# Two edge passes of a graph kernel: the block numbers of a chunk read into PE registers once instead of twice

## The chip, the cores and the metric

The kernel runs on one core of a Trainium2 chip, as one program from input to output. The metric is the device time of one execution in microseconds (us), lower is better. A core has five engines that run side by side, each with its own stream of instructions and its own sequencer, and meet only through semaphores: PE (TensorE, matmuls), DVE (VectorE), ACT (ScalarE), POOL (GpSimd, here above all the gathers) and SP (SyncE, which issues the plain DMAs).

## The reference

The program is a two-layer model on a graph of 6250 nodes, 256 features and 106,250 edges sorted by their target node. Each layer has a graph stage and a feed-forward stage. Two stages matter here. They have the same form: a score for every edge and head, a softmax of the scores over the edges of one target node, and a sum of messages, weighted with it, into that node.

```python
# layer 0: attention
score = einsum('ehd,ehd->eh', K[src], Q[dst]) / sqrt(HD) + edge_bias
m = segment_max(score, dst);  ex = exp(score - m[dst])
attn = ex / segment_sum(ex, dst)[dst]
out = segment_sum(attn[:, :, None] * V[src], dst)
# layer 1: the same with another score
scores = leaky_relu(s_src[src] + s_dst[dst], 0.2)
out = segment_sum(hh[src] * alpha[:, :, None], dst)
```

## The kernel before, in words

The nodes lie in blocks of 128. The edges are cut into **steps**: a step is a tile of 128 edges together with one block of target nodes, so that its sum goes into one block. There are 880 steps, in 55 **chunks** of 16 (`CH`), a chunk in four **quarters** of 4 steps. Which block a step belongs to is data: an earlier stage writes the numbers into `g.step_block`, one row of 32-bit integers in SBUF. An engine that needs them reads them into registers with `step_range` and computes an address from each.

Pass 1 is `attend_edges` (layer 0), pass 2 is `edges` (layer 1). Both run the same pipeline over the chunks. In one turn three chunks are under way: chunk c is scored, chunk a = c - 1 goes through the softmax, chunk b = c - 2 is multiplied out and added to its nodes. What PE does in a turn, in an order written out by hand:

- `place_t` (L440, L944) spreads the target lanes of a quarter over the partitions; ACT makes the transposed one-hot matrix `sel_t` of it (L581, L1069).
- The look-up of chunk c multiplies `sel_t` with the rows of the step's block. This is the matmul that needs a block number. In pass 1 it is `query` (L452), one for each pair of steps, eight a chunk; in pass 2 it is `at_node` (L953), one for each quarter, with four small matmuls.
- Softmax of chunk a: the scores turned (L475, L974), `row` (L479 to L481, L978 to L980), `ends` (L485, L486, L984, L985), `weights_of` (L490, L989) and the correction of what is summed so far (`at_node` L495 in pass 1, `shrinks_of` L994 in pass 2). Between them DVE scans maxima, subtracts (L750, L1231), and ACT takes the exponent (L607, L1125), copies the weights (L614, L1130), makes the one-hot matrix `sel` (L589 and L592, L1078 and L1081) and the denominators (L598, L1087).
- `add_up` of chunk b (L468, L967): one matmul of 264 columns in f32 a step, into one of two banks of PSUM in pass 1 and three in pass 2. It waits until DVE has added what stood in the bank before. DVE adds each result to its block (L785, L1266); it reads the block numbers into registers of its own, and that is not changed.

An f32 matmul shows as two records. POOL issues one gather a step (L427, L931), into a ring of 44 steps in pass 1 and of 4 chunks in pass 2, and waits until `add_up` has freed the place.

Before, PE reads the numbers in halves of eight (`U`): `blocks_of(c, half)`. The first half of chunk c + 1 is read near the end of turn c and handed to the next turn as `ahead`; the second half of chunk c is read in the middle of turn c. In pass 1 the two loads stand between `add_up(b, 10, 11)` and `add_up(b, 12, 13)`, and between `ends(a)` and `add_up(b, 4)`. In pass 2 they stand between `add_up(b, 12, 13, 14)` and `weights_of(a)`, and between `add_up(b, 6, 7)` and `add_up(b, 8)`. In the profile both are PE's sequencer's work and have no row.

## Time and profile before

| | us |
|---|---|
| time, median of 3 runs (lowest to highest) | 5473.58 (5453.67 to 5479.73) |
| span of the profiled execution | 5404.7 |
| the profiled execution's own time | not listed apart from the three above |
| PE matmuls busy | 3933.5 (73%) |
| DVE busy | 3064.0 (57%) |
| POOL busy | 2464.9 (46%) |
| ACT busy | 1859.8 (34%) |

The page lists for each engine what share of the span it was busy, and cuts the span into 40 slices. The whole span mixes stages with different limits: the two edge passes are about half of it. A timeline row gives the start of an instruction or of a merged run of equal ones, how long it took, its engine and line, what it writes and reads, and in brackets how long the engine had idled before it and who ended that. Matmul starts are recorded, their ends are modelled.

### The profile page before, as it was taken

What the parts mean: (1) busy time and instruction counts of PE and PEld (TensorE: products, weight loads), DVE (VectorE), ACT (ScalarE), POOL (GpSimd) and SP (SyncE); (2) the same over time, 40 slices, a digit from 0 to 9 for tenths busy, and PEclk for the clock granted to TensorE, in tenths of its full rate; (3) what the DMA queues carried; (4) which work ended last, traced back from release to release, by engine and by line L of the source; (5) the groups of instructions that cost most, each with busy time, mean ns of one, the idle gap of its engine ahead of it and who ended that gap; (6) DMA issues with size and microseconds to landing.
All of it is one profiled execution on the core that took longest, in us unless ns stands there. A gap on an engine that the chain in (4) does not pass through costs nothing. (4 is left out here: it accounts for less than half of the span.)

```text
span 5404.7 us, 69347 instructions
## 1 busy us (share of the span) xinstructions
PE 3933.5 (73%) x16281; PEld 2847.1 (53%) x16282; DVE 3064.0 (57%) x7623; ACT 1859.8 (34%) x5073; POOL 2464.9 (46%) x2442
## 2 busy tenths in 40 slices
PE   6867777777777659967853666666666338999999
PEld 4545555555555448856732444444444226777776
DVE  3278887878888766662154666666667773111111
ACT  1333333333333312311222444444444322333332
POOL 2256665656666450001166666666663422333332
PEclk8988988888888879977986788777887559999999
DMA  2555555555555232211173333333331451111111
GB/s 80 186 146 149 154 151 148 151 140 153 147 148 151 83 118 84 91 55 40 52 252 89 95 96 96 94 95 94 93 96 47 127 194 20 32 32 31 31 31 27
DMA packets 316127, 553.64 MB, mean 102 GB/s; under 512 B 63431, under 2 KB 213783, under 8 KB 315857
## 3 DMA queue, kind: packets, MB, share of 16 engines
q0 software_dynamic: 137120, 388.63, 27.4%
q1 hardware_dynamic: 178736, 161.98, 9.8%
q8 instruction: 100, 1.64, 0.1%
q14 instruction: 171, 1.39, 0.1%
HBM read 459.75 MB, written 90.62 MB: 102 GB/s over the span
## 5 line engine op out<-in xcount | busy, mean ns | idle before, releaser
L427 POOL DMA_INDIRECT attend_ring<-kv_rows,all_step_src x880 | 860.1, 977 | 624.5 <-PE attend_ps_agg L468 371.3
L931 POOL DMA_INDIRECT edge_ring<-head_rows,all_step_src x880 | 878.7, 999 | 457.1 <-issue 204.2
L967 PE MATMUL edge_ps_agg<-edge_msg,edge_sel 128*128 128x264 f32 x1760 | 676.3, 520 | 188.9 <-issue 57.3
L468 PE MATMUL attend_ps_agg<-attend_msg,attend_sel 128*128 128x264 f32 x1760 | 605.1, 445 | 179.7 <-DVE graph_qa L785 122.9
L967 PEld LDWEIGHTS edge_ps_agg<-edge_msg,edge_sel 128*128 128x128 f32 x1760 | 414.5, 257 | 328.2 <-issue 198.7
L1266 DVE TENSOR_TENSOR graph_acc<-graph_acc,edge_ps_agg 128x264 f32 x880 | 369.9, 420 | 367.2 <-PE edge_ps_agg L967 169.0
L2821 DVE TENSOR_TENSOR moe_gl<-moe_ps_h,moe_act 128x341 f32<-128x341 f32 x210 | 107.8, 514 | 776.8 <-PE moe_ps_h L2739 776.8
L452 PE MATMUL attend_ps_q<-graph_qa,attend_sel_t 128*128 x1760 | 527.7, 429 | 27.4 <-ACT attend_sel_t L581 17.8
L785 DVE SCALAR_TENSOR_TENSOR graph_qa<-graph_qa,all_step_same,attend_ps_agg 128x264 f32 x880 | 421.1, 479 | 170.1 <-remote 121.0
L468 PEld LDWEIGHTS attend_ps_agg<-attend_msg,attend_sel 128*128 128x128 f32 x1760 | 329.3, 208 | 347.2 <-issue 148.6
L2739 PE MATMUL moe_ps_h<-experts_w,moe_xt 128*128 x1680 | 501.7, 451 | 0.6 <-ACT moe_xt L2770 0.6
L589 ACT ACTIVATE attend_sel<-all_lane,all_step_dst 128x128 f32<-128x128 f32 x880 | 281.1, 390 | 498.5 <-PE attend_ps_agg L468 232.4
L2693 POOL DMA_INDIRECT out<-moe_y,moe_to_row x105 | 166.8, 1588 | 579.4 <-ACT moe_y L2779 567.5
L452 PEld LDWEIGHTS attend_ps_q<-graph_qa,attend_sel_t 128*128 128x128 f32 x1760 | 377.0, 217 | 99.7 <-issue 31.6
L2739 PEld LDWEIGHTS moe_ps_h<-experts_w,moe_xt 128*128 128x128 f32 x1680 | 311.1, 190 | 146.4 <-issue 2.8
L1254 DVE TENSOR_TENSOR edge_msg<-edge_ring,edge_prob 128x256 f32<-128x256 f32 x880 | 345.1, 414 | 32.0 <-issue 17.6
L1069 ACT ACTIVATE edge_sel_t<-edge_ps_gt 128x512 bf16<-128x512 f32 x220 | 130.5, 593 | 576.5 <-DMA tab_rel_x<-tab_rel_x 402.8
L1078 ACT ACTIVATE edge_sel<-all_lane,all_step_dst 128x128 f32<-128x128 f32 x880 | 279.1, 389 | 125.4 <-PE edge_ps_agg L967 86.6
L680 DVE TENSOR_TENSOR attend_prod<-attend_ps_q,attend_ring 128x512 f32<-128x512 f32 x440 | 297.7, 677 | 40.8 <-remote 30.2
L2724 PE MATMUL moe_ps_y<-experts_w,moe_gt 128*128 x1260 | 309.9, 387 | 0.7 <-ACT moe_gt L2796 0.7
L1825 PE MATMUL ffn_ps_h<-ffn_xt,ffn_wa 128*128 128x256 f32 x1216 | 272.3, 383 | 11.8 <-ACT ffn_xt L1848 11.8
L1867 ACT ACTIVATE ffn_ht<-ffn_ps_h,ffn_ba 128x256 f32<-128x256 f32 x304 | 144.2, 474 | 364.2 <-PE ffn_ps_h L1825 364.2
(424 smaller groups left out, 6587.9 us busy)
## 6 DMA issues: line engine op xcount, KB each, us to landing
attend_ring<-kv_rows,all_step_src POOLq DMA_INDIRECT x880
edge_ring<-head_rows,all_step_src POOLq DMA_INDIRECT x880
kv_rows<-qkv_kv SPq DMA_DIRECT2D x25, 512.0 KB, 2.9
experts_w<-in_w_t SPq DMA_DIRECT2D x16, 682.0 KB
attend_mask<-run_starts SPq DMA_DIRECT2D x440, 8.1 KB
edge_mask<-run_starts SPq DMA_DIRECT2D x440, 8.1 KB
head_rows<-hds_hh SPq DMA_DIRECT2D x25, 264.0 KB
qkv_x<-in_x SPq DMA_DIRECT2D x25, 256.0 KB, 3.3
```

The source lines that it names most:

```text
L427: nc.gpsimd.indirect_dma_start(ring[:, step % RING1, :], None, g.kv_rows, bass.IndirectOffsetOnAxis(g.step_src[:, step:step + 1], 0)).then ...
L452: ins = nc.tensor.matmul(ps_q[k % QBANKS][:, i, :], sel_t[:, q % 2, u % QU, :], queries[:, bass.ds(blocks[u % U], 1), :].rearrange("p b d ...
L468: nc.tensor.matmul(ps_agg[i % SUM_BANKS][:, 0:AGG], sel[:, q % 2, u % QU, :], msg[:, q % 2, u % QU, :], start=True, stop=True).then_inc(s_ ...
L589: ins = nc.scalar.activation(sel[:, q % 2, u, :], g.lane[:], ACT.Square, bias=g.step_dst[:, step:step + 1], scale=-1.0)
L680: nc.vector.tensor_tensor(prod[:, at:at + 2, :], ps_q[k % QBANKS][:], ring[:, first:first + 2, 0:D], ALU.mult).then_inc(s_prod, 1)
L785: nc.vector.scalar_tensor_tensor(at[u % U], at[u % U], g.step_same[:, i:i + 1], ps_agg[i % SUM_BANKS][:, 0:AGG], ALU.mult, ALU.add).then_i ...
L931: nc.gpsimd.indirect_dma_start(ring[:, n % slots, u, :], None, g.head_rows, bass.IndirectOffsetOnAxis(g.step_src[:, step:step + 1], 0)).th ...
L967: nc.tensor.matmul(ps_agg[i % BANKS][:, 0:AGG], sel[:, q % 2, u % QU, :], msg[:, q % 2, u % QU, :], start=True, stop=True).then_inc(s_agg, 1)
L1254: nc.vector.tensor_tensor(msg[:, q % 2, u % QU].rearrange("p (h c) -> p h c", c=HC)[:, :, 0:HD], ring[:, b % slots, u, 0:D].rearrange("p ( ...
L1266: nc.vector.tensor_tensor(at[u % U], at[u % U], ps_agg[i % BANKS][:, 0:AGG], ALU.add).then_inc(s_add, 1)
L2724: last = nc.tensor.matmul(ps_y[:], gt[0:size, c, :], w2[0:size, :, c, :][:, bass.ds(e, 1), :].rearrange("p a d -> p (a d)"), start=(c == 0 ...
L2739: last = nc.tensor.matmul(ps_h[2 * i + hf][:, 0:EHALF], xt[:, slot, k, :], w13[:, :, k, i, hf * EHALF:(hf + 1) * EHALF][:, bass.ds(e, 1), ...
```

## The change

Both passes: `blocks_of` takes no half any more and reads all 16 numbers of a chunk; a look-up takes its number by the step's own place in the chunk and not by its place in the half. One call a turn is left, for chunk c + 1. In pass 1 it stands after the last query of the turn (`query(c, 7, ...)`), ahead of `add_up(b, 10)`. In pass 2 it stands after the last look-up (`at_node(c, 3, ...)`), ahead of `place_t(c + 1, 0)`. The order of all else is the same. The 16 registers are held until the last look-up of the next turn.

```diff
--- before.py
+++ after.py
@@ -450,7 +450,7 @@
                 for i in range(2):
                     u = pair * 2 + i
                     ins = nc.tensor.matmul(ps_q[k % QBANKS][:, i, :], sel_t[:, q % 2, u % QU, :],
-                                           queries[:, bass.ds(blocks[u % U], 1), :].rearrange("p b d -> p (b d)"), start=True, stop=True)
+                                           queries[:, bass.ds(blocks[u], 1), :].rearrange("p b d -> p (b d)"), start=True, stop=True)
                 ins.then_inc(s_q, 1)
 
             def add_up(b, *steps):
@@ -494,14 +494,14 @@
                 pe.wait_ge(s_rs, a * quarters + 1)
                 nc.tensor.matmul(shrinks, sel[:, 0, 0, :], shrink[:], start=True, stop=True).then_inc(s_shrink, 1)
 
-            def blocks_of(c, half):
-                return step_range(nc, g, mybir.EngineType.PE, c * CH + half * U, U)
+            def blocks_of(c):
+                return step_range(nc, g, mybir.EngineType.PE, c * CH, CH)
 
             pe.wait_ge(s_set, SET_OPS)
             pe.wait_ge(s_made, 2)
             place_t(0, 0)
             place_t(0, 1)
-            ahead = blocks_of(0, 0)
+            ahead = blocks_of(0)
             query(0, 0, ahead)
             query(0, 1, ahead)
 
@@ -522,35 +522,31 @@
                     query(c, 3, ahead)
                 if a is not None:
                     ends(a)
-                if c is not None:
-                    blocks = blocks_of(c, 1)
                 if b is not None:
                     add_up(b, 4)
                 if c is not None:
-                    query(c, 4, blocks)
+                    query(c, 4, ahead)
                     place_t(c, 3)
                 if b is not None:
                     add_up(b, 5, 6)
                 if a is not None:
                     weights_of(a)
                 if c is not None:
-                    query(c, 5, blocks)
+                    query(c, 5, ahead)
                 if b is not None:
                     add_up(b, 7)
                 if c is not None:
-                    query(c, 6, blocks)
+                    query(c, 6, ahead)
                 if after:
                     place_t(c + 1, 0)
                 if b is not None:
                     add_up(b, 8, 9)
                 if c is not None:
-                    query(c, 7, blocks)
+                    query(c, 7, ahead)
+                if after:
+                    ahead = blocks_of(c + 1)
                 if b is not None:
-                    add_up(b, 10, 11)
-                if after:
-                    ahead = blocks_of(c + 1, 0)
-                if b is not None:
-                    add_up(b, 12, 13)
+                    add_up(b, 10, 11, 12, 13)
                 if after:
                     query(c + 1, 0, ahead)
                     place_t(c + 1, 1)
@@ -951,7 +947,7 @@
                 pe.wait_ge(s_rt, c * quarters + q + 1)
                 for u in range(QU):
                     ins = nc.tensor.matmul(ps_sd[:, q * QU + u].rearrange("p h a -> p (h a)"), sel_t[:, q % 2, u, :],
-                                           dst_parts[:, bass.ds(blocks[(q * QU + u) % U], 1)].rearrange("p b h a -> p (b h a)"),
+                                           dst_parts[:, bass.ds(blocks[q * QU + u], 1)].rearrange("p b h a -> p (b h a)"),
                                            start=True, stop=True)
                 ins.then_inc(s_sd, 1)
 
@@ -993,18 +989,17 @@
                 pe.wait_ge(s_rs, a * quarters + 1)
                 nc.tensor.matmul(shrinks, sel[:, 0, 0, :], shrink[:], start=True, stop=True).then_inc(s_shrink, 1)
 
-            def blocks_of(c, half):
-                return step_range(nc, g, mybir.EngineType.PE, c * CH + half * U, U)
+            def blocks_of(c):
+                return step_range(nc, g, mybir.EngineType.PE, c * CH, CH)
 
             pe.wait_ge(s_set, SET_OPS)
             pe.wait_ge(s_made, 3)
-            for half in range(2):
-                blocks = blocks_of(0, half)
-                for q in (2 * half, 2 * half + 1):
-                    place_t(0, q)
-                    at_node(0, q, blocks)
+            blocks = blocks_of(0)
+            for q in range(quarters):
+                place_t(0, q)
+                at_node(0, q, blocks)
             place_t(1, 0)
-            ahead = blocks_of(1, 0)
+            ahead = blocks_of(1)
 
             def turn(c, a, b, ahead):
                 after = c is not None and c + 1 < count
@@ -1025,26 +1020,21 @@
                 if a is not None:
                     row(a)
                 if b is not None:
-                    add_up(b, 6, 7)
-                if c is not None:
-                    blocks = blocks_of(c, 1)
-                if b is not None:
-                    add_up(b, 8)
+                    add_up(b, 6, 7, 8)
                 if a is not None:
                     ends(a)
                 if c is not None:
-                    at_node(c, 2, blocks)
+                    at_node(c, 2, ahead)
                     place_t(c, 3)
                 if b is not None:
                     add_up(b, 9, 10, 11)
                 if c is not None:
-                    at_node(c, 3, blocks)
+                    at_node(c, 3, ahead)
                 if after:
+                    ahead = blocks_of(c + 1)
                     place_t(c + 1, 0)
                 if b is not None:
                     add_up(b, 12, 13, 14)
-                if after:
-                    ahead = blocks_of(c + 1, 0)
                 if a is not None:
                     weights_of(a)
                 if b is not None:
```

## Rows read from the trace of the kernel before

**Rows 1.** Stages: start:end, length, each engine's busy time, granted clock, DMA.

```profile
core 0: us, PE busy (x) PEld busy (x) DVE busy (x) ACT busy (x) POOL busy (x), PEclk, DMA share, GB/s
...
290.00:1830.00 1540.00, 1115.18 (x4317) 797.89 (x4317) 1245.24 (x2617) 591.92 (x1657) 929.91 (x896) 0.88 0.53 147
...
2900.00:4190.00 1290.00, 840.80 (x3511) 555.00 (x3509) 854.19 (x2665) 584.81 (x1680) 815.36 (x815) 0.79 0.34 90
```

**Rows 2.** Once a turn, by line: count, duration min/median/max, first and last start.

```profile
L490 PE MATMUL attend_ps_tp<-all_ident,attend_prob_t x55: 327/328/477, 294.1 to 1840.2; 128*128 128x128 f32 x55
...
L989 PE MATMUL edge_ps_tp<-all_ident,edge_prob_t x55: 272/418/476, 2892.5 to 4168.9; 128*128 128x128 f32 x55
```

**Rows 3.** Timeline of PE, opening of pass 2.

```profile
2824.05 0.70 PE L953 MATMUL edge_ps_sd<-edge_dst_parts,edge_sel_t 128*128 x4 [0.77 <-ACT edge_sel_t L1069]
2825.23 0.59 PE L944 MATMUL edge_ps_gt<-edge_feat,all_lane_feat 128*128 128x512 bf16 x1 [0.48 <-issue]
2826.59 0.57 PE L953 MATMUL edge_ps_sd<-edge_dst_parts,edge_sel_t 128*128 x4 [0.77 <-ACT edge_sel_t L1069]
2827.01 0.59 PE L944 MATMUL edge_ps_gt<-edge_feat,all_lane_feat 128*128 128x512 bf16 x1
```

**Rows 4.** Timeline of PE, one turn of pass 1.

```profile
1002.25 0.69 PE L468 MATMUL attend_ps_agg<-attend_msg,attend_sel 128*128 128x264 f32 x2
...
1010.01 1.03 PE L452 MATMUL attend_ps_q<-graph_qa,attend_sel_t 128*128 x4
1010.88 0.61 PE L468 MATMUL attend_ps_agg<-attend_msg,attend_sel 128*128 128x264 f32 x2
...
1013.03 1.32 PE L468 MATMUL attend_ps_agg<-attend_msg,attend_sel 128*128 128x264 f32 x4 [0.38 <-DVE graph_qa L785]
```

**Rows 5.** Timeline of DVE, the same turn.

```profile
1012.41 0.48 DVE L785 SCALAR_TENSOR_TENSOR graph_qa<-graph_qa,all_step_same,attend_ps_agg 128x264 f32 x1
```

**Rows 6.** Timeline of PE, one turn of pass 2.

```profile
3644.32 2.85 PE L967 MATMUL edge_ps_agg<-edge_msg,edge_sel 128*128 128x264 f32 x6
...
3647.64 0.38 PE L944 MATMUL edge_ps_gt<-edge_feat,all_lane_feat 128*128 128x512 bf16 x1
```

**Rows 7.** PE by line, 2900 to 4190 us: busy, mean, idle before.

```profile
L944 PE MATMUL edge_ps_gt<-edge_feat,all_lane_feat 128*128 128x512 bf16 x210 | 99.3, 473 | 0.2
```

**Rows 8.** Timeline of all engines, end of a turn of pass 2.

```profile
3629.32 0.56 PE L953 MATMUL edge_ps_sd<-edge_dst_parts,edge_sel_t 128*128 x4 [3.61 <-ACT edge_sel_t L1069]
...
3629.91 0.38 PE L944 MATMUL edge_ps_gt<-edge_feat,all_lane_feat 128*128 128x512 bf16 x1
...
3630.14 2.83 PE L967 MATMUL edge_ps_agg<-edge_msg,edge_sel 128*128 128x264 f32 x6
...
3631.39 0.39 DVE L1266 TENSOR_TENSOR graph_acc<-graph_acc,edge_ps_agg 128x264 f32 x1
3631.72 0.27 DVE L1231 TENSOR_TENSOR edge_less<-edge_ps_tp,edge_most 128x128 f32<-128x128 f32 x1
3632.02 0.31 ACT L1125 ACTIVATE edge_prob_t<-edge_less 128x128 f32<-128x128 f32 x1 [1.10 <-DVE edge_less L1231]
...
3632.76 0.42 PE L989 MATMUL edge_ps_tp<-all_ident,edge_prob_t 128*128 128x128 f32 x1
...
3636.40 1.39 PE L967 MATMUL edge_ps_agg<-edge_msg,edge_sel 128*128 128x264 f32 x4 [1.74 <-issue]
```

**Rows 9.** Timeline of ACT, the turn of rows 6.

```profile
3652.38 0.60 ACT L1069 ACTIVATE edge_sel_t<-edge_ps_gt 128x512 bf16<-128x512 f32 x1 [3.68 <-DMA tab_rel_x<-tab_rel_x]
```

**Rows 10.** ACT by line: 2900 to 4110 us, then 4110 to 4190 us.

```profile
L1069 ACT ACTIVATE edge_sel_t<-edge_ps_gt 128x512 bf16<-128x512 f32 x202 | 119.8, 593 | 482.6 <-DMA tab_rel_x<-tab_rel_x 381.1 <-PE edge_ps_gt L944 81.1 <-issue 20.2
...
L1069 ACT ACTIVATE edge_sel_t<-edge_ps_gt 128x512 bf16<-128x512 f32 x8 | 4.7, 590 | 8.5 <-PE edge_ps_gt L944 8.4
```

**Rows 11.** The gathers of pass 2 by line, and POOL's idle before them.

```profile
L931 POOL DMA_INDIRECT edge_ring<-head_rows,all_step_src x880: 952/960/1412, 2795.9 to 4118.0; - x176
...
  PE edge_ps_agg L967: 157.6, 177
```

## The prediction

> **What bounds the kernel now.** The change touches two stages, so I read the stage table first and not the whole span. Pass 1, `attend_edges`, fills 290 to 1830 us and pass 2, `edges`, fills 2900 to 4190 us; in pass 1 DVE is busy 1245 of 1540 us and PE 1115, in pass 2 no engine is above two thirds [rows 1]. Each pass runs 55 turns, and an operation that runs once a turn gives the turn: (1840.2 - 294.1) / 54 = 28.6 us in pass 1 and (4168.9 - 2892.5) / 54 = 23.6 us in pass 2 [rows 2]. Pass 2 is therefore a chain across engines, where one microsecond added at the right place costs 50. Then I read the timeline of PE around each of the four places where block numbers are read, and beside it DVE and ACT.
>
> A register load is not an instruction that the profile counts as busy, so it shows only as a hole on PE, where nothing covers it. The opening of pass 2 has one such hole. The opening does place, look up, place, look up for the four quarters of chunk 0. Where no load stands between look-up (L953) and place (L944), place starts 2827.01 - 2826.59 = 0.42 us after look-up. Where the second load of eight stands, it starts 2825.23 - 2824.05 = 1.18 us after, with 0.48 us of it marked idle [rows 3]. **A load of eight registers pushes back what follows by about 0.75 us.** It is the same seam (L953, load, L944) at which the change puts its new load in pass 2.
>
> **Pass 1, load removed after `ends`.** It stands between L486 and step 4's L468. PE's L468 at 1002.25 has no idle before it [rows 4]: the sequencer reads registers while PE still works off what is queued, the queries ahead of `ends` above all. Nothing is gained; without that cover the load would have cost 0.75 us.
>
> **Pass 1, load removed between steps 11 and 12.** PE idles 0.38 us before step 12's L468 at 1013.03, released by DVE's L785 [rows 4]. DVE adds step 10 from 1012.41 for 0.48 us, and only its end (1012.89) frees the bank of step 12; DVE did not idle before it [rows 5]. So the load is hidden by DVE, and 0 is gained. Bound below zero: if the 0.38 us were the load's after all, 53 x 0.38 = 20 us.
>
> **Pass 1, new load of 16 between query 7 and step 10.** Query 7 keeps PE from 1010.01 until step 10 starts at 1010.88 (0.87 us of cover), and DVE takes step 10 at 1012.41, 0.92 us after PE ended it at 1010.88 + 0.61 = 1011.49 [rows 4, 5]. A load that pushes back by 0.75 to 1.5 us shows up to 0.6 us on PE and none of it on DVE. Step 11 waits for DVE's add of step 9, which the load doesn't touch. Cost 0. Pass 1 in sum: 0, bounds -20 and +10 (0.2 us a turn, if some turns lack the cover).
>
> **Pass 2, load removed between steps 7 and 8.** PE runs steps 6, 7, 8 as one block of 2.85 us from 3644.32 with no idle in it [rows 6]: in all that time two matmuls a step are queued and the load runs beside them. Gain 0.
>
> **Pass 2, load removed between step 14 and `weights_of`.** PE runs steps 12, 13, 14 as one block of 2.83 us from 3630.14, then L989 at 3632.76 without idle [rows 8]. Gain 0.
>
> **Pass 2, new load of 16 between the last look-up and `place_t(c + 1, 0)`.** Here PE has no cover: look-up (L953) at 3629.32 follows an idle of 3.61 us, and L944 (3629.91) and step 12 (3630.14) follow it without a gap [rows 8]; over the stage L944 waited 0.2 us in 210 runs [rows 7]. So the whole push-back appears. For 16 registers it is at least the 0.75 us of eight and at most twice that, 1.5 us; no row here splits the 0.75 us into a fixed part and a part per register. I take 1.1, the middle. What is queued behind the load on PE: L944, steps 12 to 14, L989, step 15, L994. Who waits:
> - ACT's L1069, which answers L944; the next on ACT is L1125 (3632.02), after 1.10 us idle and itself later by then, so this is covered.
> - DVE's add of step 12, at 3631.39. A third of PE's block of 2.83 us is one step, so step 12 is done at 3630.14 + 0.94 = 3631.08 and DVE has it 0.3 us later [rows 8]. Part of the 0.3 is the signal's way, so the cover is 0 to 0.3 us; I take 0.2. Where the clock is granted in full the steps are done sooner and the cover is larger; its mean here is 0.79 [rows 1].
> - Behind that add, in DVE's fixed order, stands L1231 (3631.72), for which ACT idled 1.10 us (L1125, 3632.02). ACT then has two one-hot groups, `prob` and the denominators to make, and for these PE's first step of the next turn (3636.40) idles 1.74 us [rows 8]. Nothing on this chain has slack.
>
> So each turn grows by 1.1 - 0.2 = 0.9 us. 52 turns have both the load and a chunk being added: 52 x 0.9 = 47 us. Bounds: 52 x (0.75 - 0.3) = 23 and 52 x 1.5 = 78 us. The openings trade two loads of eight for one of 16, under 1 us. The number of address calculations, of matmuls and of DMAs is the same.
>
> The Trainium skill, "Runtime: NRT & Kernel Launch", section "Instruction fetch mechanics", gives about 200 ns for each register loaded, also in bulk; by it eight would take 1.6 us and 16 3.2 us. The row's 0.75 us for eight speaks against that size here, though that page speaks of loads from HBM. "DMA: Bandwidth & Descriptors", section "Latency and other measured facts", gives a floor of about 600 ns for a load; if the load were all floor, the new one would push back by the 0.75 us of the old, and the sum would be its lower bound.
>
> **Sum.** Span 5404.7 + 47 = 5451.7 us. The profiled execution's own time is not listed; the three runs lie 49 to 75 us above its span. I set the sum on the median: 5473.6 + 47 = 5520.6 us.
>
> **Rivals.**
> 1. *Absorbed, no change.* Twice a turn ACT and DVE idle for a signal of PE that comes long after the work: L944 runs at 3647.64 for 0.38 us, but ACT's L1069 starts at 3652.38 after 3.68 us idle [rows 6, 9]. Such waits (the name "tab_rel_x" in the row is a wrong guess of the releaser) are 381.1 us of ACT's idle in 202 runs of L1069 [rows 10]. In the last turns, after the last gather was issued at 4118.0, L1069 idles 8.5 us in 8 runs and never for that name [rows 10, 11]. So these waits belong to the gathers and not to PE's own order. If their end is set by the gathers' pace, 0.9 us more in front of them only shortens them: 0 to 15 us in all, 5480. For it: no row explains them. Against it: L931 itself idles for PE 157.6 us [rows 11], so gathers follow PE, and the chain from the look-up at 3629.32 to the next turn at 3636.40 lies outside them [rows 8].
> 2. *Twice the price.* The 16 numbers come as two loads, or the time goes with the count: 52 x (1.5 - 0.2) = 68 us, 5541.
> 3. *Faster: one late signal goes with one load.* The late signal at 3652.38 follows the first look-up after the load between steps 7 and 8 [rows 6, 9], and there are two loads and about two such waits a turn. If the load is their cause, one of two goes, from the turn in which the second load is gone: half of 381.1 = 190 us less, and 47 more, 5330. Against it: the last turns have both loads and hardly any late signal [rows 10]. Its mild form is that the 20 us of pass 1 are real and pass 2 is absorbed: 5454.
>
> **How the numbers follow.** Forecast (23 to 60 us slower) 0.47; absorbed 0.27; twice the price or pass 1 hit too 0.12; mild gain 0.10; a late signal gone 0.04. 0.5% is 27 us, about what a measurement can tell from no change. The forecast's lower end lies inside it, which gives slower 0.57, within 0.33, faster 0.10. The range takes in the mild gain in part and the double price: 5460 to 5555. The forecast alone spans 5497 to 5534.
>
> **What would show each step.** In pass 2's opening, and after each last look-up, L944 with an idle of about 1 us that was not there: the new load; its length is the price. L989 from first to last 47 us longer, its 55 runs 24.5 us apart. The idle before ACT's L1125 up from 1.1 to 2.0 us. In pass 1, L490 first to last the same within 10 us, and L468 at step 12 still idle 0.38 us for L785. The forecast is wrong if the waits at L1069 shrink by what L944 gains, or if L944's new idle is under 0.5 us.

## The result, and the profile after

The kernel after takes 5454.36 us (median of 20 runs, 5419.99 to 5469.84), the kernel before 5469.55 us (20 runs, 5453.67 to 5496.9). The ratio is 0.9969, with a 95% interval of 0.9955 to 0.9982: 17 us less (10 to 25). I had forecast 5520.6 us, 47 us more, and a range from 5460 to 5555. The sign was wrong and the time lies below the range.

The profiled execution of the kernel after has a span of 5465.8 us, that of before 5404.7 us. So the two profiles differ by 61 us in the direction opposite to the timed runs. Below, ten more profiled executions with pass 1 unchanged on slower chips give 1572 to 1599 us for L490 from first to last, where that of before gave 1546 [rows 2]. Its span lies below every timed run of before. **The recorded profile of before was a quick execution**, and the lengths of stages in it can't be set against those of after. What can be compared is the form of a turn.

The kernel after, once a turn (columns: count, duration min/median/max, first and last start):

```profile
L490 PE MATMUL attend_ps_tp<-all_ident,attend_prob_t x55: 327/332/478, 295.6 to 1880.5; 128*128 128x128 f32 x55
L985 PE MATMUL edge_ps_tp<-all_ident,edge_prob_t x55: 272/338/476, 2931.1 to 4230.3; 128*128 128x128 f32 x55
```

Pass 2 takes 4230.3 - 2931.1 = 1299.2 us against 1276.4 [rows 2]. L985 is L989 of before; the lines of pass 2 lie 4 lower on PE, 10 lower on ACT and DVE. The end of a turn of pass 2, timeline of PE, DVE and ACT after:

```profile
3509.11 0.57 PE L949 MATMUL edge_ps_sd<-edge_dst_parts,edge_sel_t 128*128 x4 [4.44 <-ACT edge_sel_t L1059]
...
3510.77 0.59 PE L940 MATMUL edge_ps_gt<-edge_feat,all_lane_feat 128*128 128x512 bf16 x1 [1.09 <-issue]
3511.15 2.85 PE L963 MATMUL edge_ps_agg<-edge_msg,edge_sel 128*128 128x264 f32 x6
...
3512.38 0.43 DVE L1256 TENSOR_TENSOR graph_acc<-graph_acc,edge_ps_agg 128x264 f32 x1 [1.13 <-PE edge_ps_agg L963]
...
3512.73 0.28 DVE L1221 TENSOR_TENSOR edge_less<-edge_ps_tp,edge_most 128x128 f32<-128x128 f32 x1
3513.05 0.31 ACT L1115 ACTIVATE edge_prob_t<-edge_less 128x128 f32<-128x128 f32 x1 [1.05 <-DVE edge_less L1221]
```

It is the place of [rows 8]. The new load stands there as 1.09 us of idle on PE, and DVE now waits 1.13 us for step 12. From the look-up to the exponent it is 3513.05 - 3509.11 = 3.94 us, where it was 3632.02 - 3629.32 = 2.70 us. It is not this turn alone: over the 52 turns of each trace the distance has a median of 2.79 us before and 3.95 us after, a mean of 3.06 and 3.84. At this place the forecast of 0.9 us a turn came nearly true. The whole pass did not follow. Two more groups of after, 2900 to 4190 us (PE) and 2900 to 4110 us (ACT); the last column is the idle time before the group:

```profile
L940 PE MATMUL edge_ps_gt<-edge_feat,all_lane_feat 128*128 128x512 bf16 x155 | 78.8, 508 | 32.2 <-issue 32.2
L1059 ACT ACTIVATE edge_sel_t<-edge_ps_gt 128x512 bf16<-128x512 f32 x194 | 115.1, 593 | 467.3 <-DMA tab_rel_x<-tab_rel_x 255.1 <-PE edge_ps_gt L940 124.6 <-issue 87.6
```

L940's idle was 0.2 us [rows 7] and is 32.2 (a quarter of its records is missing here). ACT's waits for PE's late signals, 381.1 us before [rows 10], are down to 255.1. In pass 1, the turn of [rows 4]:

```profile
1036.43 0.68 PE L468 MATMUL attend_ps_agg<-attend_msg,attend_sel 128*128 128x264 f32 x2
1037.45 0.71 PE L468 MATMUL attend_ps_agg<-attend_msg,attend_sel 128*128 128x264 f32 x2 [0.34 <-issue]
1038.54 1.32 PE L468 MATMUL attend_ps_agg<-attend_msg,attend_sel 128*128 128x264 f32 x4 [0.38 <-DVE graph_qa L781]
```

Step 12 still waits 0.38 us for DVE's L781. From step 10 to step 12 it is 2.11 us, before 1013.03 - 1010.88 = 2.15. The 0.34 us before step 11 is not the new load, since the kernel before idles there too, and longer:

```profile
1011.95 0.71 PE L468 MATMUL attend_ps_agg<-attend_msg,attend_sel 128*128 128x264 f32 x2 [0.46 <-issue]
```

The trace also holds records of the loads themselves, which no view prints. The new one runs from 1035.15 for 1.12 us, while PE works off steps 8 and 9 and query 7, so it is hidden nearly whole: step 10 starts 0.91 us after query 7, where it was 0.87. The removed one ran from 1011.95 for 0.59 us, beside step 11, and ended 0.49 us before step 12 started.

### The profile page after: what moved, and what is told of

The parts are those of the page before. It is cut to its first block and busy times, and to the rows that moved or that the text cites. A ratio compares the mean times of both kernels' runs of the same rounds, so it can differ in the third digit from the quotient of the medians.

```text
span 5465.8 us, 69110 instructions
## 1 busy us (share of the span) xinstructions
PE 3936.6 (72%) x16154; PEld 2869.7 (53%) x16282; DVE 3067.4 (56%) x7623; ACT 1863.3 (34%) x5073; POOL 2451.9 (45%) x2442
## 5 line engine op out<-in xcount | busy, mean ns | idle before, releaser
L468 PE MATMUL attend_ps_agg<-attend_msg,attend_sel 128*128 128x264 f32 x1760 | 620.0, 456 | 179.3 <-DVE graph_qa L781 127.5
L452 PE MATMUL attend_ps_q<-graph_qa,attend_sel_t 128*128 x1760 | 538.9, 436 | 29.1 <-ACT attend_sel_t L577 23.2
L781 DVE SCALAR_TENSOR_TENSOR graph_qa<-graph_qa,all_step_same,attend_ps_agg 128x264 f32 x880 | 421.6, 479 | 190.8 <-remote 138.3
L452 PEld LDWEIGHTS attend_ps_q<-graph_qa,attend_sel_t 128*128 128x128 f32 x1760 | 388.3, 224 | 106.3 <-issue 32.8
L1826 PE MATMUL ffn_ps_y<-ffn_wb,ffn_ht 128*128 128x256 f32 x1216 | 268.7, 379 | 0.0
```

Of the source, the lines that this page charges most:

```text
L452: ins = nc.tensor.matmul(ps_q[k % QBANKS][:, i, :], sel_t[:, q % 2, u % QU, :], queries[:, bass.ds(blocks[u], 1), :].rearrange("p b d -> p ...
L468: nc.tensor.matmul(ps_agg[i % SUM_BANKS][:, 0:AGG], sel[:, q % 2, u % QU, :], msg[:, q % 2, u % QU, :], start=True, stop=True).then_inc(s_ ...
L781: nc.vector.scalar_tensor_tensor(at[u % U], at[u % U], g.step_same[:, i:i + 1], ps_agg[i % SUM_BANKS][:, 0:AGG], ALU.mult, ALU.add).then_i ...
```

## The experiments

The chips differ, and the runs fell on two kinds. On the **quicker** ones the kernel before takes 5030 us (e1 to e4, e17, e18), on the **slower** ones 5463 to 5470 us (e5 to e16; the recorded result too). Between e1 and e9, the same kernel on either kind, pass 2 differs by 158 us. The granted clock in it differs little (0.79 and 0.76), and PE is busy for only 25 us more (805.0 and 830.1 us, in the latter with 2% of its records missing), so the clock is not the main cause of the difference. I compare only within one kind. Each ratio is to the kernel before on the same chip, with its 95% interval.

**e1, e2: the kernel before and the whole change, for the stages.**

> The kernel before, unchanged, run as a kernel of its own: how far two equal kernels lie apart, and how a second profiled execution of it splits over the stages. The recorded profile of before has a span of 5404.7 us, below every timed run (5453.67 at least), that of the changed kernel 5465.8. If the recorded profile of before was a quick execution, this one shows pass 1 longer than its 1546 us (L490 from first to last); if profiled executions are quicker in general, it is near 5405 again. Ratio 1.000, within 0.3%.

> The whole change again, for its stages in a second profile. Theory A (the price of the load in pass 2 is paid before the turn's last steps and got back where ACT waits for PE's late signals, and pass 1 gains a little): ratio 0.997, pass 2 from first to last L985 1276 to 1300 us as in the two profiles at hand. Theory B (pass 2 pays 20 us and more, and pass 1 gains more than that): the same ratio, but the two stages move apart by 30 us or more.

Measured: e1 0.9992 (0.9982 to 1.0002), e2 0.9969 (0.9957 to 0.998), 5015.12 against 5030.63 us. The gain of the record came again, on the other kind of chip.

**e3, e4: one pass of the change at a time.** e3 takes the hunks of `attend_edges`, e4 those of `edges`.

> Only pass 1 of the change; pass 2 keeps its two loads of eight a turn. My recorded prediction gave pass 1 zero (bounds 20 us faster, 10 slower): ratio 0.996 to 1.002. Theory A: 10 to 20 us faster (the 0.38 us idle before step 12 were the load's in part), ratio 0.9965. Theory B: 30 us or more faster, ratio 0.994 or less. Theory C (the gain comes from pass 2): ratio 1.000.

> Only pass 2 of the change; pass 1 keeps its two loads of eight a turn. Recorded prediction: 47 us slower, ratio 1.0086. Theory A (absorbed at the late signals): ratio 0.999 to 1.001. Theory B (20 us and more slower, outweighed by pass 1): ratio 1.004 or more. Theory C (a gain in pass 2, because fewer stops of PE's sequencer mean fewer or shorter late signals): ratio 0.997 or less.

Measured: e3 0.9997 (0.9988 to 1.0005), e4 0.9967 (0.9956 to 0.9979). On the quicker chip all the gain is in pass 2 (theory C by its size), where I had put the loss. The profiles say the same: with the old loads pass 2 takes 1130.2 and 1129.1 us from the first L989 to the last (e1, e3), with the new one 1118.6 and 1115.1 (e2, e4). Here is why. POOL's gathers and DVE's score addition, which needs them, first e1, then e4:

```profile
L931 POOL DMA_INDIRECT edge_ring<-head_rows,all_step_src x880 | 884.3, 1005 | 286.1 <-issue 195.9 <-PE edge_ps_agg L967 71.6 <-POOLq L83 11.1
L1169 DVE TENSOR_TENSOR edge_score<-edge_dst_sum,edge_ring 128x128 f32<-128x128 f32 x55 | 20.6, 374 | 209.7 <-DMA edge_ring<-head_rows,all_step_src 209.6
```

```profile
L931 POOL DMA_INDIRECT edge_ring<-head_rows,all_step_src x880 | 869.5, 988 | 288.0 <-issue 199.6 <-PE edge_ps_agg L967 68.0 <-POOLq L83 12.8
L1163 DVE TENSOR_TENSOR edge_score<-edge_dst_sum,edge_ring 128x128 f32<-128x128 f32 x55 | 20.6, 375 | 158.3 <-DMA edge_ring<-head_rows,all_step_src 158.2
```

And the timeline of e1, POOL with DVE's multiply L1254 beside it:

```profile
3300.43 0.40 DVE L1254 TENSOR_TENSOR edge_msg<-edge_ring,edge_prob 128x256 f32<-128x256 f32 x1
3300.60 1.06 POOL L931 DMA_INDIRECT edge_ring<-head_rows,all_step_src  x1 [0.30 <-issue]
3301.08 0.42 DVE L1254 TENSOR_TENSOR edge_msg<-edge_ring,edge_prob 128x256 f32<-128x256 f32 x1
...
3301.96 0.95 POOL L931 DMA_INDIRECT edge_ring<-head_rows,all_step_src  x1 [0.30 <-issue]
...
3303.22 0.96 POOL L931 DMA_INDIRECT edge_ring<-head_rows,all_step_src  x1 [0.31 <-issue]
...
3304.48 0.95 POOL L931 DMA_INDIRECT edge_ring<-head_rows,all_step_src  x1 [0.30 <-PE edge_ps_agg L967]
...
3305.54 0.41 DVE L1254 TENSOR_TENSOR edge_msg<-edge_ring,edge_prob 128x256 f32<-128x256 f32 x1
3305.74 1.04 POOL L931 DMA_INDIRECT edge_ring<-head_rows,all_step_src  x1 [0.31 <-PE edge_ps_agg L967]
```

POOL issues one gather behind the other with 0.30 us between them, whatever releaser the row names. (884.3 + 286.1) / 880 = 1.33 us a gather with the opening, 16 of them a turn: **on the quicker chip the turn is POOL's**, and DVE waits 209.7 / 54 = 3.9 us a turn for the data. The new load's 1.1 us fits into that wait, which falls to 158.3. The floor of a turn is 16 x (0.305 + 0.956) = 20.2 us; the turns took 20.98 us (e1) and 20.65 (e4), and the difference is all in the gathers' own durations, 16.10 and 15.77 us a turn. A gather is longer when DVE's multiply L1254 runs beside its start, as at 3300.60 and 3305.74. Over 704 gathers of e1 those with an L1254 in their first 0.35 us (292) took 1.057 us, the others 0.971; in e4 1.015 (286) and 0.966. So in e4 DVE's multiplies meet the gathers at less costly moments. L1254 reads two inputs from SBUF. The Trainium skill, "GPSIMD Engine Reference", section "Specifications", says that GpSimd shares its SBUF interfaces with VectorE and contends with VectorE's instructions that have two SBUF inputs; the rows agree. What this is worth, 0.33 us a turn x 52 = 17 us, is the gain of e4 (16 us). The forecast had no such term. I take it for luck of phases, but that is not shown: the mean gather is 987 to 993 ns in every run with another order of loads in pass 2 and the full multiply, on both kinds of chip (e5, with the load at the old place, and e8, without one, among them), and 994 to 1005 ns in every run with the old order. Which part of the edit moves the multiplies was not isolated on a quicker chip.

**e5 to e8: where the load stands, how many loads, and none** (slower chip; pass 1 as before).

```diff
 # e5
                 if after:
-                    ahead = blocks_of(c + 1)
                     place_t(c + 1, 0)
                 if b is not None:
                     add_up(b, 12, 13, 14)
+                if after:
+                    ahead = blocks_of(c + 1)
 # e6
-                return step_range(nc, g, mybir.EngineType.PE, c * CH, CH)
+                return [x for half in range(2) for x in step_range(nc, g, mybir.EngineType.PE, c * CH + half * U, U)]
 # e7
-                    ahead = blocks_of(c + 1)
+                    for _ in range(3):
+                        ahead = blocks_of(c + 1)
 # e8
-                    ahead = blocks_of(c + 1)
```

> Pass 1 as before. In pass 2 one load of 16, but at the old place between step 14 and `weights_of`; the load between steps 7 and 8 is gone. Theory G (POOL issues the 16 gathers of a turn without a pause, 0.305 us and at least 0.956 us each, so the turn is 20.2 us and what DVE's multiplies add to single gathers; PE's loads count only by where they shift those multiplies): ratio 0.994 to 1.003, and the turn again equals POOL's busy time plus 16 gaps. Theory M (the gain is that of the load removed between steps 7 and 8): ratio 0.997 or less, L931's turn at 20.7 us or less against 20.98. Theory P (the gain is the new place): ratio 1.000 or more.

> Pass 1 as before. In pass 2 two loads of eight, one behind the other, at the new place. Theory G: as with one load of 16 (ratio 0.9967), within 0.002. The hole on PE before L944 is 1.1 us with one load of 16; with two of eight 1.2 us. Theory M or P: the same. Theory S (one instruction less for PE's sequencer is the gain): ratio 0.999 to 1.001.

> Pass 1 as before. In pass 2 the load of 16 stands three times at the new place, which pushes back PE by 2 x 1.1 = 2.2 us more a turn. Recorded prediction (each us at this place lengthens the turn): 52 x 2.2 = 114 us above one load, ratio 1.019. Theory G: DVE's wait for the gathers at the score addition (L1169 of before) is 158 us in 54 turns = 2.9 us a turn with one load and takes up the 2.2 us: 0 to 20 us above one load, ratio 0.996 to 1.001, and that wait falls to 40 to 60 us in all.

> Pass 1 as before. Pass 2 looks every chunk's node values up with the block numbers of chunk 1, read once: none of PE's loads is left in its turns (the output is not the reference's). What all loads of pass 2 cost: theory G: nothing but shifts of DVE's multiplies, ratio 0.993 to 1.002, the turn still POOL's busy time plus 16 gaps. Recorded prediction: its new load of 1.1 us gone again, at or just below before, ratio 0.998 to 1.000. A chain over PE in which loads count in full: 2 x 0.6 us less a turn than before, 62 us, ratio 0.988.

Measured: e5 0.9999 (0.9986 to 1.0012), e6 1.0023 (1.0004 to 1.0041), e7 1.0004 (0.999 to 1.0018), e8 1.0008 (0.9992 to 1.0025). In e7 two of the three loads were never used and were not in the program that ran, so it is only another run of e4's kernel. **Without any load in its turns (e8, which uses the numbers of chunk 1 for every chunk) pass 2 is no shorter**: loads on PE are not what its turn is made of. e6 is 0.2% slower than before, with an interval that just excludes 1; its hole, 0.12 us longer than that of one load, would make 6 us of the 13. L944's holes were 1.11 us with one load of 16 and 1.23 with two of eight, as expected. Theories M, P and S say where the gain of the quicker chip comes from. On this kind of chip pass 2 gains nothing in any of the four, so these runs do not decide between them. Theory G's bound (POOL without a pause) is not right for it either, since POOL idles 8 to 9 us a turn there instead of 4.9.

**e9 to e12: controls, and a narrow multiply** (slower chip). The edit of e11 (on before) and e12 (on e4); both also zero `msg` once at the start, since three quarters of its columns are not written any more:

```diff
-nc.vector.tensor_tensor(msg[:, q % 2, u % QU].rearrange("p (h c) -> p h c", c=HC)[:, :, 0:HD],
-                        ring[:, b % slots, u, 0:D].rearrange("p (h d) -> p h d", h=H),
-                        prob[:, b % 2, :, u].unsqueeze(2).to_broadcast([P, H, HD]), ALU.mult).then_inc(s_msg, 1)
+nc.vector.tensor_tensor(msg[:, q % 2, u % QU].rearrange("p (h c) -> p h c", c=HC)[:, :, 0:HD // 4],
+                        ring[:, b % slots, u, 0:D].rearrange("p (h d) -> p h d", h=H)[:, :, 0:HD // 4],
+                        prob[:, b % 2, :, u].unsqueeze(2).to_broadcast([P, H, HD // 4]), ALU.mult).then_inc(s_msg, 1)
```

> The kernel before once more, for its stages beside the next three on the same chip. So far two chips were seen: the kernel before takes 5030 us on one, 5463 to 5470 us on the other. Ratio 1.000. On the quicker chip L989 from first to last is 1130 us as in the first control; on the slower one theory D (the recorded profile of before was a quick execution) says 1295 to 1305 us and pass 1's L490 1580 to 1600 us, against 1276 and 1546 in the recorded profile; if that profile was typical, these two values come again.

> Only pass 2 of the change, again. On the quicker chip: ratio 0.9967 again, POOL's turn 20.65 us. On the slower chip: theory G (the turn is not set by PE's loads at all; there it is POOL's gathers plus waits for PE's late signals): ratio 0.997 to 1.001, L989 from first to last within 8 us of the control. Recorded prediction: ratio 1.0086, 47 us more than the control.

> The kernel before, but DVE's message multiply in pass 2 (L1254) makes only a quarter of each head's columns, 64 of 256 a step (the output is not the reference's); nothing else is shortened. Theory G with its cause (a gather is held up when this multiply runs in its first 0.35 us, by 0.13 us on average): the gather's mean falls from 1006 ns to 975 or less; on the quicker chip the turn falls with it, from 20.98 to 20.5 us or less, ratio 0.994 or less. If the long gathers have another cause, their mean stays at 1000 or more, ratio 0.998 to 1.001. If instead the chain over DVE sets the turn, 16 x 0.25 = 4 us a turn could go, ratio 0.96.

> Pass 2 of the change with the same narrow multiply (64 of 256 columns a step; the output is not the reference's). Theory G: the gain of the change was the multiplies' shift against the gathers; with little left to shift, this equals the narrow kernel with the old loads within 0.1%. If the gain comes from PE's loads themselves, this one is 0.3% (16 us) below it again.

Measured: e9 0.9996 (0.9981 to 1.0011), e10 1.0006 (0.9993 to 1.0018), e11 0.9998 (0.9982 to 1.0013), e12 0.9988 (0.9971 to 1.0005). POOL's gathers in e9 and e11:

```profile
L931 POOL DMA_INDIRECT edge_ring<-head_rows,all_step_src x880 | 877.0, 997 | 472.6 <-issue 208.2 <-PE edge_ps_agg L967 161.2 <-remote 84.5
```

```profile
L931 POOL DMA_INDIRECT edge_ring<-head_rows,all_step_src x880 | 849.2, 965 | 508.5 <-issue 198.6 <-PE edge_ps_agg L967 182.1 <-remote 107.0
```

The narrow multiply takes the mean gather from 997 to 965 ns (975 or less was expected), some 32 of the 40 ns that it lay above an undisturbed one: the cause of most of the long gathers is shown. On the slower chip the 28 us come back as 36 us more idle and the time stays. Whether it would bring the 0.7% on a quicker chip was not seen, since both runs with it (e11, e16) are from slower ones. e12 is 0.1% below e11 with overlapping intervals, which decides nothing between the two expectations for it. Once a turn, e9 and e10:

```profile
L989 PE MATMUL edge_ps_tp<-all_ident,edge_prob_t x55: 272/417/477, 2920.4 to 4208.7; 128*128 128x128 f32 x55
```

```profile
L989 PE MATMUL edge_ps_tp<-all_ident,edge_prob_t x55: 273/417/477, 2932.4 to 4232.8; 128*128 128x128 f32 x55
```

1288.3 and 1300.4 us: 12 us more in these two profiles (theory G had 8 at most), 7 us in the timed medians of the two kernels. Neither is clear of the spread between equal kernels: the old pass 2 took 1276.4, 1288.3 and 1303.3 us in three profiles (before, e9, e14), the new one 1299.2, 1300.4, 1306.7 and 1310.2 (after, e10, e7, e13). The prediction had 47.

**e13 to e16: the whole, pass 1, three loads that are all used, and the narrow multiply again** (slower chip).

```diff
 # e15, on e4
-                    ahead = blocks_of(c + 1)
+                    ahead = [blocks_of(c + 1) for _ in range(3)]
+                    ahead = ahead[0][0:4] + ahead[1][4:8] + ahead[2][8:16]
```

> The whole change. On the quicker chip 0.9969 again. On the slower chip: theory R (the recorded gain there is a small real one, from pass 1): ratio 0.996 to 0.998 and e14 the same. Theory N (on the slower chip the change does nothing that repeats): ratio 0.999 to 1.001.

> Only pass 1 of the change. On the quicker chip 0.9997 again. On the slower chip: theory R: ratio 0.996 to 0.998. Theory N, and the recorded prediction for pass 1 (zero): ratio 0.999 to 1.001.

> Pass 1 as before. In pass 2 the 16 numbers are loaded three times at the new place, and each quarter's look-ups use another set, so that all three loads stay in the program: 2.1 us more on PE at that place in each of 52 turns, a hole of 3.2 us before L944 instead of 1.1. Recorded prediction (no slack on the chain): 52 x 2.1 = 109 us above one load, ratio 1.020. Theory G (other waits of the turn shrink by what the load adds): on the quicker chip 0 to 20 us above one load, ratio 0.996 to 1.001, with the wait of DVE's score addition for the gathers down from 158 us by up to 110; on the slower chip ratio 0.999 to 1.005.

> The kernel before, with DVE's message multiply of pass 2 on 64 of 256 columns a step (the output is not the reference's). On the slower chip 0.9998 again: its turn does not follow POOL's busy time. On the quicker chip (theory G): gathers without the hold-ups, POOL's turn 16 x (0.305 + 0.965) = 20.3 us against 20.98, 36 us less over the pass, ratio 0.993.

Measured: e13 0.9987 (0.9967 to 1.0007), e14 0.9981 (0.9963 to 0.9999), e15 1.0052 (1.0028 to 1.0076), e16 1.0003 (0.9985 to 1.0021). The gain of the whole is smaller here than on record, and the intervals overlap; what there is on this kind of chip comes with pass 1 (10 us of e14; 1 us on the quicker chip). e16 repeats e11: the mean gather is 965 ns again and the time stays. e15 shows how the time goes with the number of loads. L944 and ACT's L1064 in e15, then ACT in e9 and e10 (2900 to 4180 us):

```profile
L944 PE MATMUL edge_ps_gt<-edge_feat,all_lane_feat 128*128 128x512 bf16 x150 | 74.6, 498 | 127.2 <-issue 127.2
L1064 ACT ACTIVATE edge_sel_t<-edge_ps_gt 128x512 bf16<-128x512 f32 x200 | 119.1, 595 | 527.2 <-DMA tab_rel_x<-tab_rel_x 184.7 <-PE edge_ps_gt L944 175.2 <-issue 166.7
```

```profile
L1069 ACT ACTIVATE edge_sel_t<-edge_ps_gt 128x512 bf16<-128x512 f32 x210 | 124.7, 594 | 549.0 <-DMA tab_rel_x<-tab_rel_x 395.0 <-PE edge_ps_gt L944 91.4 <-issue 62.5
```

```profile
L1063 ACT ACTIVATE edge_sel_t<-edge_ps_gt 128x512 bf16<-128x512 f32 x206 | 122.4, 594 | 510.4 <-DMA tab_rel_x<-tab_rel_x 294.0 <-PE edge_ps_gt L944 138.7 <-issue 77.5
```

The unnamed waits go from 395.0 us with no load at the new place to 294.0 with one and 184.7 with three. Single runs scatter by some 65 us, but the order holds for all: 329.5 to 395.0 us in the five with no load there (before, e5, e8, e9, e14), 212.7 to 304.2 us in the five with 16 registers loaded there (after, e6, e7, e10, e13), 184.7 in e15. Part of what they lose stands in the same rows under other names: the waits for L944 grow from 91.4 to 138.7 and 175.2 us. The distance from the last look-up to the exponent grows with the loads, 3.16, 3.79 and 5.22 us (means of 52 turns of e9, e10 and e15). Yet the 109 us of loads that e15 was to have beyond e10's (52 x 2.1, the estimate from e4's hole) made some 25 us of time (1.0052 against 1.0006, on two chips, good to about 15 us): **60 to 90% are given back**, and a single load nearly whole. That is rival 1's mechanism, for this kind of chip.

**e17, e18: no gathers from chunk 4 on, without and with pass 2 of the change** (quicker chip).

```diff
+                    if n < slots:
                         nc.gpsimd.indirect_dma_start(ring[:, n % slots, u, :], None, g.head_rows,
                                                      bass.IndirectOffsetOnAxis(g.step_src[:, step:step + 1], 0)
                                                      ).then_inc(landed[n % slots], 16)
+                    else:
+                        pool.sem_inc(s_stale, 1)
...
-                v.wait_ge(landed[a % slots], (a // slots + 1) * (16 * CH))
+                if a < slots:
+                    v.wait_ge(landed[a % slots], (a // slots + 1) * (16 * CH))
+                else:
+                    v.wait_ge(s_stale, (a - slots + 1) * CH)
```

> The kernel before, but pass 2 gathers only chunks 0 to 3; later chunks use what lies in the ring (the output is not the reference's). PE's, ACT's and DVE's work is unchanged. If the gathers set the turn on both kinds of chip (POOL's issue on the quicker one, the waits for late signals of PE on the slower one), all turns take what the last ones take today, 17.2 to 17.6 us: on a slower chip 50 x (24.2 - 17.4) = 340 us less, ratio 0.938; on the quicker one 50 x (21.0 - 17.3) = 185 us less, ratio 0.963; and ACT's waits before L1069 for the unnamed releaser vanish. If the late signals are PE's own, the slower chip keeps them: turn 22 us or more, ratio 0.98 or more.

> The same without gathers from chunk 4 on, with pass 2 of the change. Against e17: recorded prediction (nothing on the chain has slack): 0.9 us a turn, 47 us slower. Theory H (the two removed loads had a price where no gather hides them, about as large as the new one's): within 15 us of e17. Theory S (the new load goes ahead of look-ups that must wait anyway): 15 to 30 us slower.

Measured: e17 0.9621 (0.9602 to 0.964), e18 0.9644 (0.9627 to 0.9661). e17 is 191 us below before (185 expected): the gathers set the turn on the quicker chip. What they hide on the slower one was not tried. e18 is 4854.67 - 4841.69 = 13.0 us above e17, 0.25 us a turn. This is the change's price on the bare chain, where I had put 0.9 us. It lies in theory H's range, but H's reason, that the two removed loads had cost about as much as the new one, is not what the rows show: the new load itself shows for only 0.28 us. The end of a turn, first e17, then e18:

```profile
3113.76 0.25 PE L957 MATMUL edge_ps_sd<-edge_dst_parts,edge_sel_t 128*128 x4
...
3114.13 1.37 PE L971 MATMUL edge_ps_agg<-edge_msg,edge_sel 128*128 128x264 f32 x4
...
3115.65 0.47 DVE L1231 TENSOR_TENSOR_SCAN edge_most<-edge_mask,edge_carry,edge_fwd 128x128 f32<-128x128 f32 x1
...
3116.04 0.39 DVE L1273 TENSOR_TENSOR graph_acc<-graph_acc,edge_ps_agg 128x264 f32 x1
3116.36 0.27 DVE L1238 TENSOR_TENSOR edge_less<-edge_ps_tp,edge_most 128x128 f32<-128x128 f32 x1
...
3116.67 0.31 ACT L1129 ACTIVATE edge_prob_t<-edge_less 128x128 f32<-128x128 f32 x1 [1.76 <-DVE edge_less L1238]
```

```profile
3105.47 0.36 PE L957 MATMUL edge_ps_sd<-edge_dst_parts,edge_sel_t 128*128 x4
...
3106.94 0.38 PE L948 MATMUL edge_ps_gt<-edge_feat,all_lane_feat 128*128 128x512 bf16 x1 [1.11 <-issue]
3107.17 1.57 PE L971 MATMUL edge_ps_agg<-edge_msg,edge_sel 128*128 128x264 f32 x6
...
3108.00 0.43 DVE L1267 TENSOR_TENSOR graph_acc<-graph_acc,edge_ps_agg 128x264 f32 x1 [0.18 <-PE edge_ps_agg L971]
...
3108.66 0.31 ACT L1123 ACTIVATE edge_prob_t<-edge_less 128x128 f32<-128x128 f32 x1 [0.71 <-DVE edge_less L1232]
```

From look-up to exponent: 3116.67 - 3113.76 = 2.91 us and 3108.66 - 3105.47 = 3.19, 0.28 more (the medians of 52 turns are 2.91 and 3.08). In e17 PE starts step 12 at about 3114.13 and DVE takes it at 3116.04, because DVE first has its own scans and multiplies to do. The load eats that cover and shows only its last 0.2 to 0.3 us.

## Why the prediction was wrong, step by step

- **A load of eight pushes back by 0.75 us, one of 16 by 0.75 to 1.5, 1.1 taken: right.** The hole is 1.09 to 1.11 us, and L940 starts 3510.77 - 3509.11 = 1.66 us after the look-up, where it was 0.59.
- **Pass 1, three edits at zero, bounds -20 and +10: within its bounds.** 0.9997 on a quicker chip, 0.9981 on a slower one (10 us less, the interval reaching nearly to 1). Step 12's idle stayed 0.38 us for DVE, as said. The new load, for which up to 0.6 us on PE was allowed, moves step 10 by 0.04 us. Where those 10 us come from no profile shows: L490 from first to last varies by 27 us between equal kernels.
- **Pass 2, removed loads at zero:** the bare chain bears this out: new load 0.28 us at its place, the whole turn 0.25.
- **The cover of the new load, 0.2 us: right for the chip of the record, wrong for the chain by itself.** I read it from one turn [rows 8], in which the last look-up followed an idle of 3.61 us. DVE had run dry in that wait too, so its add of step 12 stood right behind PE. On the slower chips it is so in most turns, and there the push-back shows whole (medians 2.81 and 3.97 us from look-up to exponent, e9 and e10). On the quicker chip about half of it shows (2.86 and 3.40, e1 and e4). In e17, where nothing waits for late signals, DVE is 1 us and more behind PE at this point, and the price is 0.25 us a turn and not 0.9.
- **"Nothing on this chain has slack": the step that failed.** It is a statement on a chain that closes once a turn, and I showed only that its last part has no gap. The turn is closed elsewhere: on the quicker chip by POOL's gathers (20.2 us and their hold-ups), on the slower one by something that comes with late signals of PE. The push-back happened at its place (look-up to exponent from 2.70 to 3.94 us in one turn, from 3.06 to 3.84 in the mean), and the turn did not grow by it: the waits for late signals shrank. So 52 x 0.9 = 47 us is what the place shows and not what the kernel pays: on the slower chips pass 2 of the change costs some 3 us, not clear of nothing (1.0006 and 1.0004 for the same kernel, e10 and e7), and on the quicker one, where the new holes before L944 add up to 59.3 us in e4, the time falls by 16 us. I had this as rival 1 at 0.27; its number, 5480, was still 26 us too high. What I held against it, that gathers wait for PE's steps, shows only that the loop runs through both.
- **Rival 3's mild form** (pass 1 gains, pass 2 absorbed, 5454 us) has the measured time, and on the slower chip its two parts have the right signs (0.9981 and 1.0006), but the reason that it gave, the 0.38 us before step 12, did not go away. It hit by size, not by cause.
- **The sum** was set on the median and not on the span, which was right; the profile's lengths of stages would have misled by 61 us. That 5404.7 + 47 = 5451.7 us lies near the measured time is luck: a base too low by some 60 us and a price too high by about as much.
- **What would show it:** "the waits at L1069 shrink by what L944 gains" stood there as the sign of a wrong forecast, and e9, e10 and e15 show it for the unnamed ones. The idle before ACT's L1125, forecast to go from 1.1 to 2.0 us, stayed (1.05; the median of 52 turns is 1.06 us in both traces). Why it stayed was not looked into.

**What stays open.** What delays PE's signals on the slower chips (3 to 4 us, about twice a turn, none on the quicker ones), and why a turn there is 24.2 to 24.6 us with one load, none, two or narrow multiplies (23.9 in the recorded profile of before). The gathers were not taken away on such a chip. And whether the 0.3% of the record is all real there: a second comparison gave 0.9987 with 1 inside its interval.

## What to carry to other kernels

Before pricing an addition on a loop's critical part, find what closes the loop: add up the busy time and fixed gaps of each engine over one turn, and look at the one whose gaps are all equal; here equal gaps of 0.30 us under different releasers were the sign of an engine at its limit. A cover must be read from several turns and best from one without a disturbance: here DVE had run dry behind a long wait of 3.61 us, and its cover looked like nearly nothing. A stall that appears in full at its place says nothing on the time until the wait that shrinks for it has been looked for.

## What the runs showed of the hardware

- One program takes 5030 us on some chips and 5465 on others; pass 2 from first to last L989 is 1130 and 1288 us (e1, e9). On the slower ones the waits of ACT for an unnamed releaser appear (395.0 us in e9), on the quicker ones there are none in the turns (e1).
- A load of 16 registers into PE makes a hole of 1.11 us, two of eight 1.23 us. The loads' own records last 0.59 us for 8 registers and 1.10 us for 16 (e1 and e4): between these two the price goes nearly with the count.
- An indirect gather's issue on POOL takes 0.956 us and 0.305 us to the next. With DVE's two-input multiply on SBUF in its first 0.35 us it takes 1.057 us on average in e1 and 1.015 in e4; with that multiply narrowed to a quarter the mean of all gathers falls from 997 to 965 ns (e9, e11).
